# Reordering the first stage: yT's low part ahead of the mask sum, three transfers begun by ScalarE instead of SyncE

## What is computed

```python
x = x + attn_ref(cond_ref(x, cond_1024, mask, ...), Wq, bq, Wk, bk, Wv, bv, gamma, beta)
x = x + ffn_ref(cond2_ref(x, cond_1024, Wx, Wh, b), w_gate, w_up, w_down)

# cond_ref, per head: 65 keys, the first from the image
scores = q @ k.T / 4 ; masked (causal, attention_mask) ; softmax ; out = attn @ v ; out @ c_proj_w
# attn_ref
ctx = relu(q) @ (relu(k).T @ v) / max(relu(q) . sum(relu(k)), 1e-6)
y = ctx + x_in ; (y - mean) / sqrt(var + 1e-5) * gamma + beta
```

## Time and profile before

| | before |
|---|---|
| median of 3 runs | 953.55 us |
| the profiled execution, device time | 955.28 us |
| its span in the profile | 953.6 us |
| PE busy | 766.9 us (80%) |
| DVE busy | 747.1 us (78%) |
| ACT busy | 429.5 us (45%) |
| POOL busy | 436.2 us (46%) |
| mean granted TensorE clock | 0.926 of full |

### The profile page before, as it was taken

One profiled execution on the slowest core, in us unless ns is written; L12 is line 12 of the kernel. 1 busy time (PEld: TensorE's weight loads), 2 busy tenths in 40 slices (PEclk: granted clock), 3 DMA queues, 4 the chain that ended last, 5 costly groups with the idle time before them and its releaser, 6 DMA issues.

```text
span 953.6 us, 23040 instructions
## 1 busy us (share of the span) xinstructions
PE 766.9 (80%) x7494; PEld 466.0 (49%) x7494; DVE 747.1 (78%) x1773; ACT 429.5 (45%) x1145; POOL 436.2 (46%) x596
## 2 busy tenths in 40 slices
PE   3347677778888778887767799999999999999965
PEld 1124454445455444554444455555555556555633
DVE  6177878667777778777744689999999999999883
ACT  2054656556665666665553333333333333333320
POOL 0054777666766667766742033322233333222332
PEclk9767989889998999999898999999999999999987
DMA  5965656676665666666620023323332333233332
GB/s 120 185 168 98 113 112 105 124 130 132 131 128 122 133 127 139 132 138 127 119 56 23 17 48 59 66 58 67 64 64 59 67 59 64 60 66 64 65 64 63
DMA packets 262383, 89.04 MB, mean 93 GB/s; under 512 B 233266, under 2 KB 261298, under 8 KB 262325
## 3 DMA queue, kind: packets, MB, share of 16 engines
q1 hardware_dynamic: 262324, 88.25, 46.7%
HBM read 25.19 MB, written 8.47 MB: 35 GB/s over the span
## 4 chain that ended last, share of the span: by engine, by line
PE 29%; DVE 17%; POOL 11%; issue 10%; SPq 9%; DMA 6%; ACT 4%; POOLq 0%; DVEq 0%; ACTq 0%
PE bank L783 10%; PE bank L920 8%; PE bank L931 5%; DVE x_value L170 4%; DMA qkT<-qk 4%; SPq L540 3%; POOL p L658 2%; DVE ffn_room L1530 2%; DVE ffn_room L1526 2%; POOL prob L651 2%; PE bank L1000 2%; PE bank L911 2%; POOL zg_rows L685 1%; SPq L568 1%; POOL x_rows_sb L692 1%
## 5 line engine op out<-in xcount | busy, mean ns | idle before, releaser
L783 PE MATMUL bank<-gu,xqT 128*128 128x512 f16 (+1 forms) x576 | 128.5, 371 | 8.6 <-DMA xqT<-xq_split 8.6
L729 POOL TENSOR_TENSOR ffn_room<-prob,h_coarse 128x704 f16<-128x704 f32 x32 | 44.1, 1377 | 154.4 <-DVE prob L171 154.4
L920 PE MATMUL bank<-wx,x1T 128*64 128x512 f16 x768 | 97.9, 392 | 2.9 <-DMA x1T<-x_split 2.9
L931 PE MATMUL bank<-wh,h 128*64 128x512 f16 x768 | 96.0, 386 | 0.7 <-ACT h L1190 0.7
L651 POOL TENSOR_TENSOR prob<-prob,row_max 128x520 f32<-128x520 f32 x64 | 68.8, 1075 | 50.7 <-DVE row_max L1355 50.7
L783 PEld LDWEIGHTS bank<-gu,xqT 128*128 128x128 f16 x576 | 56.2, 102 | 69.2 <-issue 12.2
L920 PEld LDWEIGHTS bank<-wx,x1T 128*64 128x64 f16 x768 | 79.4, 203 | 13.5 <-DMA x1T<-x_split 3.7
L1009 PE MATMUL bank<-dn,hqT 128*128 128x256 f16 x576 | 70.0, 277 | 7.6 <-DMA hqT<-ffn_room 6.6
L658 POOL TENSOR_TENSOR p<-prob,p 128x512 f16<-128x512 f32 x64 | 72.0, 1125 | 1.2 <-ACT p L1088 1.2
L1009 PEld LDWEIGHTS bank<-dn,hqT 128*128 128x128 f16 x576 | 54.7, 99 | 26.5 <-issue 18.3
L931 PEld LDWEIGHTS bank<-wh,h 128*64 128x64 f16 x768 | 41.5, 111 | 42.0 <-issue 12.1
(11 more groups left out here) (193 smaller groups left out, 1869.5 us busy)
## 6 DMA issues: line engine op xcount, KB each, us to landing
vimg_in<-image_values SPq DMA_DIRECT2D x32, 136.0 KB, 3.1
x_in<-in_x_columns SPq DMA_DIRECT2D x16, 256.0 KB, 2.9
x_res<-in_x SPq DMA_DIRECT2D x16, 256.0 KB, 3.0
x_rows<-x_rows_sb SPq DMA_DIRECT2D x32, 128.0 KB, 1.8
ffn_room<-x_rows SPq DMA_DIRECT2D x64, 64.0 KB, 2.2
out<-ffn_room SPq DMA_DIRECT2D x64, 64.0 KB, 2.0
add_mask<-in_mask_Bx1x1xS_ff SPq DMA_DIRECT2D x2, 512.0 KB, 7.6
qkT<-qk SPq DMA_TRANSPOSE x64, 4.2
```

The source lines that it names most:

```text
L729: pool.tensor_tensor(blocks(hq_split[:, 0], FF), blocks(fp4_h.value, FF), spread(h_coarse, FF), ALU.mult).then_inc(s["hq_hi"], 1)
L783: last = pe.matmul(dst, lhs(a, c), rhs(b, c), start=first and c == 0 and a == b, stop=c == C - 1 and (a, b) == parts3[-1], skip_group_chec ...
L920: last = pe.matmul(bank[e][B * h:B * h + B, :], x1T16[m][:, c, :, at], half_cols(wx16, a, c, h), start=False, stop=True, skip_group_check= ...
L931: last = pe.matmul(bank[e][B * h:B * h + B, :], h16[:, m, c, :], half_cols(wh16, a, c, h), start=False, stop=True, skip_group_check=True)
```

## The change

On **SP**, the load of x's columns, the load of x's rows and the store of x1 leave the queue; ACT starts them. The image values are loaded for one tile in every step, at the head of the step, in place of two tiles in every other step behind the transposes of p. The transpose of x1 comes one step later (a sixth tile, t6), between the transposes of qk and those of p.

On **ACT**, the load of x's columns (even tiles) or of x's rows (odd ones) is started right after the copies of qk. exp of the second half comes behind onT's high part. x1's high part moves from before y's copy to behind yT's high part, and the store of x1 follows it.

On **DVE**, yT's low part comes ahead of `masked(t1, 0)`, and `maxima` of that half right behind it at the end of the same step (before: at the head of the next). The statistics move to the next step: L1445 after `x_lo`, L1453 after the low parts of qk. x1's low part moves to the step after, behind `maxima(t2, 1)` and ahead of the seed.

On **POOL**, the variance and its power move to the next step, behind the copy of the image keys; the sum that makes x1 moves behind both `probs_lo`.

```diff
@@ SP
+        def image_values(t):
+            hold(sp, s["img_part"], t.count(2, 2, back=2), "sp_passed")
+            for b in range(2):
+                sp.dma_start(vimg_in[64 * b:64 * b + 64, t.parity].rearrange("p h c -> p (h c)"),
+                             vimg_sides[b][t.number()].partition_broadcast(S)).then_inc(vimg_loaded, 16)
...
-            if t1 and t1.parity == 0 and (t1.loop is not None or t1.b < NT - 2):
-                sp.wait_ge(s["xT_lo"], t1.count(2))
-                sp.dma_start(x_in[:, :, :], x_cols_pairs[t1.pair() + 1]).then_inc(x_loaded, 16)
+            if t1 and (t1.loop is not None or t1.b > 0):
+                image_values(t1)
             if t1:
                 ... (the two transposes of qk)
-            if t2:
-                probs_turn(t2, 0)
-                probs_turn(t2, 1)
...
-                if t1.parity == 0:
-                    hold(sp, s["img_part"], t1.count(2, 2, back=1), "sp_passed")
-                    ... (image values of two tiles)
-            if t5:
-                hold(sp, s["x1_lo"], t5.count(), "sp_passed")
+            if t6:
+                hold(sp, s["x1_lo"], t6.count(), "sp_passed")
                 ... (transpose of x1)
-                sp.dma_start(x1_tiles[t5.number()], x1_rows[:, t5.parity, :]).then_inc(x1_stored[t5.parity], 16)
-            if t3 and t3.parity == 0:
-                after(sp, s["xb_ready"], t3.count(back=1))
-                sp.dma_start(x_res[:, :, :], x_pairs[t3.pair()]).then_inc(xres_loaded, 16)
+            if t2:
+                probs_turn(t2, 0)
+                probs_turn(t2, 1)
@@ POOL (t5: after the copy of the image keys; before: t4, at the end of the step)
+                pool.wait_ge(s["mean_ready"], t5.count())
+                pool.tensor_tensor(var_eps[:, :], mean_var[:, 1:2], eps_ln[:, :], ALU.add).then_inc(s["var_ready"], 1)
+                pool.wait_ge(s["var_ready"], t5.count())
+                pool.tensor_tensor(rstd[:, :], var_eps[:, :], neg_half[:, :], ALU.pow).then_inc(s["rstd_ready"], 1)
...
+            if t2:
+                probs_lo(t2, 0)
+                image_part(t2, 1)
+                probs_lo(t2, 1)
             if t5: ... (x1 = zg + xb)
@@ ACT
+            if t1 and t1.parity == 0 and (t1.loop is not None or t1.b < NT - 2):
+                act.wait_ge(s["xT_lo"], t1.count(2))
+                act.dma_start(x_in[:, :, :], x_cols_pairs[t1.pair() + 1]).then_inc(x_loaded, 16)
+            if t4 and t4.parity == 0:
+                after(act, s["xb_ready"], t4.count(back=1))
+                act.dma_start(x_res[:, :, :], x_pairs[t4.pair()]).then_inc(xres_loaded, 16)
...
                 probs_hi(t2, 0)
-                exp(t2, 1)
             if t3:
                 hi(t3, onT16[:, 0, :], bank[0][:, 0:D], "onT_ps", "onT_hi", "y_ps")
+            if t2:
+                exp(t2, 1)
... (behind yT's high part)
+                act.wait_ge(s["x1_ready"], t5.count())
+                after(act, s["x1T_in"], t5.count(per=16, nth=16, back=1))
+                act.copy(x1_split[:, 0, :], x1_rows[:, t5.parity, :]).then_inc(s["x1_hi"], 1)
+                act.dma_start(x1_tiles[t5.number()], x1_rows[:, t5.parity, :]).then_inc(x1_stored[t5.parity], 16)
@@ DVE
-            if t2:
-                maxima(t2, 0)
             ... (x_lo)
+            if t5:
+                dve.wait_ge(s["resid"], t5.count())
+                dve.bn_stats(stats[:, :], res_rows[:, :]).then_inc(s["stats_ready"], 1)
             ... (low parts of qk)
+            if t5:
+                passed(s["stats_ready"], t5.count())
+                passed(s["var_ready"], t5.count(back=1))
+                passed(s["neg_ready"], t5.count(back=1))
+                dve.bn_aggr(mean_var[:, :], stats[:, :]).then_inc(s["mean_ready"], 1)
             ... (masked and maxima of t2's second half)
+            if t6:
+                dve.wait_ge(s["x1_hi"], t6.count())
+                dve.tensor_tensor(x1_split[:, 1, :], x1_rows[:, t6.parity, :], x1_split[:, 0, :], ALU.subtract)\
+                    .then_inc(s["x1_lo"], 1)
             ... (behind v's low part)
-                masked(t1, 0)
-            ... (statistics of t4, and their waits)
             if t3:
                 lo(t3, yT16[:, 1, :], bank[6][:, D:2 * D], yT16[:, 0, :], "yT_hi", "yT_lo")
+            if t1:
+                masked(t1, 0)
+            if t1:
+                maxima(t1, 0)
```

More of the change, by code:

```diff
@@ L564, in step @@
                     sp.wait_ge(s["vimg_stored"], 16)
[L565 to L570 removed]
+                    image_values(t1)
                     late_loads()
[L572 to L574 removed]
+            if t6:
+                hold(sp, s["x1_lo"], t6.count(), "sp_passed")
+                sp.dma_start_transpose(x1T_all[:, :, :, bass.ds(t6.number() * 2, 2), :].rearrange("p i c b s -> p (i c) (b s)"),
                                        x1_split[:, :, :].rearrange("p i d -> p (i d)")).then_inc(s["x1T_in"], 16)
[L576 to L581 removed]
+            if t2:
+                probs_turn(t2, 0)
+                probs_turn(t2, 1)
+        pipeline(sp, 6, step, first=10)
         for q in range(2):
@@ L663, in image_part @@
             if e == 0:
-                pool.wait_ge(vimg_loaded, mask_count(t))
+                pool.wait_ge(vimg_loaded, t.count(per=32, nth=32))
                 after(pool, s["o_seeded"], t.count(back=2))
@@ L678, in step @@
                                  kimgT[:, :, bass.ds(t1.number() * 2, 2)]).then_inc(s["kimg_in"], 1)
+            if t5:
+                pool.wait_ge(s["mean_ready"], t5.count())
+                after(pool, s["rstd_ready"], t5.count(back=1))
+                after(pool, s["z_ready"], t5.count(back=1))
+                pool.tensor_tensor(var_eps[:, :], mean_var[:, 1:2], eps_ln[:, :], ALU.add).then_inc(s["var_ready"], 1)
+                pool.wait_ge(s["var_ready"], t5.count())
+                pool.tensor_tensor(rstd[:, :], var_eps[:, :], neg_half[:, :], ALU.pow).then_inc(s["rstd_ready"], 1)
             if t2:
@@ L692, in step @@
                 pool.tensor_tensor(x1_rows[:, t5.parity, :], zg_rows[:, :], xb_rows[:, :], ALU.add).then_inc(s["x1_ready"], 1)
-            if t2:
-                probs_lo(t2, 0)
-                image_part(t2, 1)
-                probs_lo(t2, 1)
             if t4:
@@ L1151, in step @@
                     .then_inc(s["v_hi"], 1)
-            if t5:
-                act.wait_ge(s["x1_ready"], t5.count())
-                after(act, s["x1T_in"], t5.count(per=16, nth=16, back=1))
-                act.copy(x1_split[:, 0, :], x1_rows[:, t5.parity, :]).then_inc(s["x1_hi"], 1)
             ffn_hi(t4, "heads", "ctx")
@@ L1356, in maxima, with passed @@
                 .then_inc(s["max_ready"], 1)
+        def passed(sem, value):
+            hold(dve, sem, value, "dve_passed")
         def ffn_lo(t4, place):
@@ L1460, in _ @@
         x_lo(Tile(None, 0))
-        pipeline(dve, 5, step, first=10)
+        pipeline(dve, 6, step, first=10)
         dve.memset(hq_split[:, :, FF:], 0.0).then_inc(s["b_zero"], 1)
```

31 lines of the change are left out of this document (5 added, 26 removed).

## The result

| | before | after |
|---|---|---|
| median, us (range, runs) | 953.17 (952.65 to 953.72, 4) | 937.90 (936.55 to 940.27, 4) |
| ratio, 95% interval | | 0.9842 (0.9821 to 0.9864) |
| profiled span, us | 953.6 | 936.5 |
| mean granted clock in that span | 0.926 | 0.918 |
| steady step (21 steps), us | 12.99 | 12.05 |

The change gains 15.3 us. It was forecast to gain 35: the time lies within the range, beyond the forecast case's own 912 to 926 and at the upper edge of rival A's 928 to 938. What A says of the port is not what happened, as the rows show.

A forecast was written before the change was run, and what follows sets the result against it. Bound: waits, from SP's queue delaying q and k's transposes in slow steps and yT's late low part in the others. Gains 31.3 (steady steps) plus 4.9 (early steps) less 1.2 (last steps), together 35 us, gave 918.5 us; range 905 to 944.

The forecast's parts named there:

- the forecast case: Whole kernel: steady step of 11.2 to 11.8 us, time 912 to 926 us; chance 0.52.
- rival A: x1's low part takes 1.35 us each step or ACT's transfers cost their cover: period 12.0 to 12.4, 928 to 938; chance 0.20.
- the first ten: First ten steps, longer by weight chores: half of 9.8 us of statistics' waits for POOL saved, 4.9 us.
- 21 steady steps: First stage: each step falls from 12.99 to 11.5 us, together 31.3 us gained.
- last marker to second stage: Last steps: x1's low part stands behind the last weight pieces; net loss 1.2 us, with 3 us either way.
- the second late thing: In the steps not slowed by SP's queue, PE waits for yT's low part: 18.1 us in 12 waits.
- x1's low part: On DVE's cycle: 0.44 us if it wins the port shared with POOL, 1.35 if not; expected to mostly win.
- PE needs pT only in the next step: End of ACT's order: p's second low part ends later, but this was taken to be harmless; no cost.
- No term: POOL: same instructions, busy 46% of the span; moved variance, power and x1's sum cost nothing.
- two cycles, DVE's and qkT's: Loops setting the step: DVE's order closes after 10.8 to 11.7 us, the transfer of q and k after 10.7.
- ACT's starts cost nothing: One load and one store per step on ACT, costed at nothing; 0.4 to 0.9 us a step if cover goes.
- rival D: PE's clock drops behind new waits before o's transposes and the projection: 2.4 us added per step, 969 us; chance 0.08.

The follow-up runs named there:

- the later store: Changed kernel with x1's store still started by ACT, but in its next step, ahead of z and away from p's transposes: 914.99 us, 0.955 of the kernel before.
- the doubled store: Changed kernel with ACT starting each x1 store a second time right behind the first, into a spare tensor: 934.96 us, 0.9798 of the kernel before.
- after's second run: The changed kernel itself, unaltered, measured again beside the kernels of another set on their chip: 936.95 us, 0.9771 of the kernel before.
- z behind: Changed kernel with POOL scaling z behind both p low parts, and ACT's exponentials and high parts of p ahead of z: 916.89 us, 0.9576.
- the first low part ahead: Changed kernel with only p's first low part ahead of z's scaling on POOL, and its high part ahead of z on ACT: 920.48 us, 0.9607.

## Why the prediction was right and wrong, point by point

**The sum.** By the two profiled spans: an earlier start of the steps 0.5 and the first ten 1.3 us (forecast 4.9 together), 21 steady steps 19.8 (31.3), last marker to second stage -3.3 (-1.2), second stage -1.2 (0): 17.1 us, against 35. The steady steps carry 11.5 of the 18 us missing. Some 10 of these are the lower clock in 8 steps, by that estimate: with these at 11.72 us, as at equal waits and a held clock, 21 steps would take 242.5 us, against 241.5 in the forecast (21 x 11.5) and 253 measured. The forecast's value for a step was met where the clock held, by luck in part, since another cycle sets it.

**Right: what bound the kernel before.** SP's queue was the bound of every second step: with it cleared and nothing else changed, nearly all steps took 12.0 us, and the time was 0.9865, by the medians more than half of what the whole change gives. In these steps PE waited for yT's low part each time, the second late thing of the prediction. Transposes of q and k no longer wait in the queue, and PE waits neither for qkT nor for yT's low part.

**Right: x1's low part.** 0.416 us, the low end. DVE starts it 0.16 us ahead of POOL's shift each time; the shift then has 1.167 us as its median, 1.057 before. The rule of the Trainium skill ("SBUF — State Buffer", section "SBUF: two separate sides"), that whoever starts first holds the pair of ports, agrees with all 23 instances. The first of rival A's two conditions is thus false, though its range, 928 to 938, and its step, 12.0 to 12.4, hold what was measured. Its second, ACT's transfers at the price of their 0.4 us of start, is false as well (with both still on ACT the later store has steps of 11.03); they did cost, but by the landing of pT.

**Wrong: "PE needs pT only in the next step", and with it "No term" for POOL.** This is the step that failed: the wait for pT and the cycle behind it stood at nothing in the sum, and measured 25.1 us of waits in 22, with some 10 us of lower clock behind them. Both sentences looked forward from one instruction and asked whether it had slack in its own step. The next step's use closes a loop: attend, `linear_kv`, k and v, z, z's scaling, p's low parts, pT, attend. Its length is the step, whatever slack each piece seems to have. Its pieces were all in the trace of before; I walked two cycles, DVE's and qkT's, and not this one. The difference itself shows POOL's wait for z ahead of p's low parts, and I did not ask who stands behind that wait, nor who waits for those.

**Wrong: ACT's starts cost nothing.** ACT's own time was costed rightly (0.37 to 0.39 us, hidden). Of the transfers I counted no shorter landing, and by the same reading should have asked about a longer one: pT's went from 3.2 to 3.8 us, and undoing that one move, or only moving it in time, is worth some 20 us (914.99 against 936.95 on one chip; 0.9599 with the store on SP), the clock's share included. The Trainium skill ("DMA: Bandwidth & Descriptors", section "Issuing engines are not separate DMA queues") says that transfers of several issuing engines share the same DMA engines; the rise of the landing agrees with that, though the doubled store shows that it isn't simply bytes.

**Partly right: rival D.** It priced the clock at 2.4 us a step, in all steps, and placed it behind waits before o's transposes and the projection. It came at the wait for pT, in 8 of 21 steps, and cost 1.35 us in each. Behind 12 of the 17 waits of 1.67 to 1.92 us `linear_kv`'s six products took 2.3 to 2.8 us, behind 5 of them 1.46. Behind the 23 waits of up to 1.56 us between 197 and 433 us in the kernel with two stores no group of products took more than 1.46. But slow products also stand behind shorter waits elsewhere: 1.46 us in after (at 437.27 us), 1.32 in its second run, 1.57 and 1.43 at 200 us in the kernels with z behind and with the first low part ahead. The length of one wait does not tell it alone.

**Sizes.** The first ten steps were to give 4.9 us and gave 1.8 with their start. From 20 to 187 us PE's waits for yT's low part, 10.3 us in 5, are gone, but those for the normalised o grew from 19.0 to 26.4 us: most of what was freed was waited for elsewhere. The last steps lost 3.3 by the profiled spans, 53.2 us against 49.9; in after's second run (439.17 to 488.82 us) they take 49.65, so that term lies within what executions differ by. The 0.1 us for a semaphore in the prediction's step is shown by no row. The second stage's wait for x1T is as foretold: in the chain the low part stands behind a weight piece.

```profile
489.91 0.96 DVE gu L483 x2
490.87 0.34 DVE x_split L1403
...
491.29 2.42 DMA x1T<-x_split
...
493.76 2.85 PE bank L918 x12
```

Moving it gave 1 us.

**What stays open.** Why a store in flight lengthens pT's landing by 0.5 to 0.6 us and a second one adds nothing. What decides, at waits of 1.67 to 1.92 us, whether the clock falls: 5 of 17 times it did not. Why odd and even steps still differ in after, now that SP's queue no longer holds back q and k; every second wait for pT is the long one, and no run isolated it. What yT's low part ahead of the mask sum is worth by itself. And whether the 0.955 of the best kernel is the order's doing alone: its clock is 1.00 against 0.95, and of its 1.0 us per step against after the two can be parted only roughly, some 0.5 us by the clock and 0.5 by the order.

## What to carry to other kernels

In a software pipeline, "needed only in the next step" is not slack: follow each late product through its use in the next step until you are back where you started, and take the longest such loop as the step. The chain of waits shows it in one look, since the same instruction comes back at the distance of a step. Of a transfer that is moved, ask which latency-bound transfer it will fly beside, and place it by time, not by queue; and look at what PE's products take behind its longest waits: here the slow ones stood there, and in one profile work of no use in the wait gave shorter steps.

## What the runs showed of the hardware that was not expected

- A plain store of 128 KB started on ACT beside a DMA transpose lengthened the transpose's way to its landing from 3.2 or 3.3 to 3.8 us (medians of some 45). Twice the store: 3.9. The same store at another time, from either engine: 3.3.
- At nearly the same sum of PE's waits for pT the granted clock differed: 25.1 us in 22, the longest 1.8, went with 0.95; 24.2 us in 23, the longest 1.6, with 1.00. A fall to the level of 1.2 GHz behind a wait cost 0.8 to 1.3 us in the six products alone (1.46 us, and 2.30 to 2.77), and 1.35 us in the step.
- More work on PE did not lengthen the steps: with 12 products more in each, the steady ones took 11.75 us on average in the one profile, against 12.05.
